# Eight-layer transformer on one core: zero rows in the nested projections, input by sequence, a late store of parts, and shifts split on GpSimd

## The chip, the cores and the metric

The kernel runs on one core of a Trainium2 chip as one program. The metric is its device time in microseconds (us), the median of several runs. The engines are PE (TensorE, matrix products), DVE (VectorE), ACT (ScalarE), POOL (GpSimd) and SP (SyncE, which issues the DMAs). In code and rows, "banks" are the eight PSUM banks that PE writes to.

## The reference

`x` holds 4 sequences of 1024 rows with 128 columns, float32. Eight layers follow one another, each `x = x + layer(layernorm(x))`: a causal attention with one head, a nested attention, a wide attention, the nested one again, a linear attention, a mixture of 8 experts, a gated recurrence and the mixture again. The change touches mostly the nested and the wide attention:

```python
def nested(x):                       # 8 heads of width 16
    for e in range(4):               # quarter e of the sequence sees m = 128, 64, 32, 16 features
        m = d // 2 ** e
        xm = layernorm(x[:, e*n:(e+1)*n])[..., :m] # with norm_w, norm_b
        q, k, v = xm @ q_w[:, :m].T + q_b, ...     # k_w, v_w the same way
    attn = softmax(q @ k.T * scale)  # all 1024 rows against all 1024 keys, per head
    out  = attn @ v                  # then xm @ o_w[:m, :m] + o_b[:m], the other columns 0
def wide(x):                         # 16 heads of width 8, no mask, no q, k, v bias
    q, k, v = x @ Wq.T / sqrt(D), x @ Wk.T, x @ Wv.T
    return softmax(q @ k.T) @ v @ Wff.T + bff
```

## The kernel before

**Frame.** `x` stays in SBUF from `load_stage` (L68, four DMAs at L73, one for each sequence) to `store_stage` (L91, four DMAs at L101). The main function runs the layers one after another. Every stage is a block of its own: an engine that enters a new block waits at a barrier until all five engines, SP among them, have left the block before.

**A layer with heads** (two nested, one wide) is three stages. `project_stage` (L413) handles the four sequences b in turn: DVE takes the statistics, POOL makes the factors of the layer norm in a chain of small instructions, DVE normalises (L545), PE turns the eight tiles (L687), ACT copies them back with norm_w and norm_b (L624), PE projects q and k (L697) and v (L704). Since float32 scores are wanted, q and k are cut into parts, two of type fp32r in the nested layers and three of type bf16 in the wide one (ACT L645 to L652, DVE L564 to L573), and SP writes the parts to DRAM (`store`, L474). In the nested layers each expert's matmuls use only m rows of weight and input: 128, 64, 32 and 16. ACT also scales `x` itself there (`grow_rows`, L635) and POOL adds the bias of the output (L519).

`attend_stage` (L717) reads the parts back, four heads (a group) at a time, to the rows of `q_stack` and `k_stack` (`Heads.load`, L398 and L402). A unit is one group and half of its rows: there are 16 units in each nested layer and 32 in the wide one, 64 in all. For a unit PE makes the plain scores (L896), DVE takes the maxima of two banks at a time (`maximum`, L797, 16 for each unit) and then the two bf16 parts of the negated row maximum (`shifts`, L804, L806, L808). PE turns these parts (`turn_shifts`, L905), ACT copies them out (L856), and SP moves them by four DMAs to two more rows of `q_stack` (L778), whose partners in `k_stack` are rows of ones. The shifted scores (L926) then come out less their maximum, ACT takes 32 exponentials (L849) and PE multiplies these with the values (L939). The maxima of a unit are taken while the exponentials of the unit before it run. `output_stage` applies the last weight (L1048 in PE).

**Order of the work.** Each engine's program is written out by hand in a fixed order, with semaphores between engines. SP issues load(0) and load(1) in the project stage after the stores of b = 0 and 1, then the stores of b = 2 and 3, and load(2) in the attend stage.

**The mixture layers** start with a chain on POOL (`Front.on_gpsimd`, L1105 to L1114), which makes the factor of the layer norm that is applied to an already normalised input.

## Time and profile before

| what | us |
|---|---|
| median of 3 runs (3285.5 to 3297.26) | 3286.0 |
| the profiled run, its own time | 3277.16 |
| its span | 3275.1 |
| load stage | 0 to 10.7 |
| first nested layer: project from, first scores at | 162.4, 245.0 |
| wide layer: project from, first scores at | 648.0, 712.8 |
| second nested layer: project from, first scores at | 1410.2, 1489.8 |
| first nested attend stage ends | 634.1 |
| mixture layers start | 2088.8 and 2851 |
| last addition ends, store is issued, span ends | 3264.6, 3265.9, 3275.1 |

PE is busy for 2907.9 us (89% of the span), DVE 2459.1, ACT 2215.6, POOL 188.5. The mean granted TensorE clock is 0.917 of full speed.

The views in the section of rows are of these kinds. In the page's clock line each digit is a slice of 81.9 us. A window row gives, for a stretch from:to, its length, then the busy time of PE, PE's weight loads, DVE, ACT and POOL, each with its number of instructions in brackets, then the granted clock, the busy share of the 16 DMA engines and GB/s. A timeline row gives start, duration, engine, line, operation and tiles with shapes and count; in brackets stands how long the engine was idle before it and what ended that. SPq is the time in which SP issues a DMA, PEld a weight load. A row by tile gives the shortest, median and longest duration in ns, and the first and last start.

### The profile page before, as it was taken

The numbers are of one execution on the slowest core, as the hardware profiler recorded it, in microseconds if no ns is written. First come the engines' busy times: TensorE is split into PE (matmuls) and PEld (weight loads), VectorE is DVE, ScalarE is ACT, GpSimd is POOL, SyncE is SP. The second block draws the span as 40 slices with busy tenths as digits, with TensorE's granted clock in tenths as the row PEclk, the third lists the DMA queues.
The fourth block names the chain that finished last, engine by engine and source line by source line (L and its number), as shares of the span: only waits on it lengthen the run. The fifth ranks groups of instructions, "written<-read, shape, count | busy, mean of one in ns | idle before, by whom it ended". The sixth has DMA issues, their size and how long they took to land. (4 is left out here: it accounts for less than half of the span.)

```text
span 3275.1 us, 53109 instructions
## 1 busy us (share of the span) xinstructions
PE 2907.9 (89%) x19734; PEld 1664.7 (51%) x19734; DVE 2459.1 (75%) x3887; ACT 2215.6 (68%) x3872; POOL 188.5 (6%) x329
## 2 busy tenths in 40 slices
PE   6868999859999999977999989799997777789998
PEld 4643444422333333353444456678885455578886
DVE  5648999479999999747999564477776777677776
ACT  2345888638888888953888722288886444378886
POOL 0030000020000000030000020100000000010000
PEclk9957999869999999966999989799998888889999
DMA  1052121030000000033221010211110000111112
GB/s 28 1 114 64 29 40 21 6 106 11 21 21 21 21 21 21 2 83 84 41 41 21 2 28 1 66 40 46 46 49 21 1 0 0 39 50 46 49 46 58
DMA packets 76838, 115.24 MB, mean 35 GB/s; under 512 B 13840, under 2 KB 38448, under 8 KB 76592
## 3 DMA queue, kind: packets, MB, share of 16 engines
q1 hardware_dynamic: 76592, 111.99, 14.5%
q8 instruction: 151, 2.47, 0.3%
q14 instruction: 95, 0.78, 0.1%
HBM read 85.73 MB, written 25.43 MB: 34 GB/s over the span
## 5 line engine op out<-in xcount | busy, mean ns | idle before, releaser
L797 DVE TENSOR_REDUCE nested_a_halves<-banks 128x2 f32<-128x1024 f32 x512 | 617.4, 1222 | 78.8 <-PE banks L896 75.6
L849 ACT ACTIVATE nested_a_p<-banks 128x512 f32<-128x512 f32 x1024 | 553.7, 597 | 117.1 <-PE banks L926 100.7
L797 DVE TENSOR_REDUCE wide_a_halves<-banks 128x2 f32<-128x1024 f32 x512 | 593.4, 1216 | 42.1 <-PE banks L896 42.1
L849 ACT ACTIVATE wide_a_p<-banks 128x512 f32<-128x512 f32 x1024 | 554.1, 598 | 44.5 <-PE banks L926 33.2
L1725 DVE TENSOR_TENSOR mix_e_h_low<-mix_e_h,mix_e_h_high 128x512 fp32r<-128x512 f32 x512 | 349.6, 688 | 174.9 <-ACT mix_e_h_high L1831 167.0
L1848 ACT ACTIVATE mix_e_h<-banks,mix_b_folded 128x512 f32<-128x512 f32 x512 | 353.8, 691 | 103.5 <-PE banks L1902 103.1
L939 PE MATMUL banks<-nested_a_p,nested_values 128*32 128x256 f32 x4096 | 326.9, 398 | 0.0
L939 PE MATMUL banks<-wide_a_p,wide_values 128*32 128x256 f32 x4096 | 321.0, 391 | 0.0
L1831 ACT ACTIVATE mix_e_h_high<-mix_e_h 128x512 fp32r<-128x512 f32 x512 | 319.3, 624 | 0.0
L896 PE MATMUL banks<-nested_k_stack,nested_q_stack 48*128 48x512 f32 x1024 | 270.8, 524 | 48.8 <-PEq L453 24.3
L926 PE MATMUL banks<-nested_q_stack,nested_k_stack 50*128 50x512 f32 x1024 | 252.3, 423 | 10.9 <-ACT nested_a_p L849 9.9
L926 PE MATMUL banks<-wide_q_stack,wide_k_stack 50*128 50x512 bf16 x1024 | 223.6, 381 | 22.6 <-ACT wide_a_p L849 19.3
L896 PE MATMUL banks<-wide_k_stack,wide_q_stack 48*128 48x512 bf16 x1024 | 205.9, 398 | 34.5 <-DVE wide_a_halves L797 18.1
L896 PEld LDWEIGHTS banks<-nested_k_stack,nested_q_stack 48*128 48x128 f32 x1024 | 102.0, 196 | 247.8 <-issue 186.7
L1902 PE MATMUL banks<-mix_x_high,mix_w_high 128*128 128x512 f32 x512 | 208.5, 407 | 0.0
L1916 PE MATMUL banks<-mix_e_h_high,mix_w_high 128*128 128x512 f32 x512 | 202.1, 395 | 6.9 <-DVE mix_e_h_low L1725 6.9
L1902 PE MATMUL banks<-mix_x_high,mix_w_low 128*128 128x512 f32 x512 | 205.1, 401 | 0.0
L1902 PE MATMUL banks<-mix_x_low,mix_w_high 128*128 128x512 f32 x512 | 203.3, 397 | 0.0
L1916 PE MATMUL banks<-mix_e_h_low,mix_w_high 128*128 128x512 f32 x512 | 203.3, 397 | 0.0
L1916 PE MATMUL banks<-mix_e_h_high,mix_w_low 128*128 128x512 f32 x512 | 201.1, 393 | 0.0
L926 PEld LDWEIGHTS banks<-nested_q_stack,nested_k_stack 50*128 50x128 f32 x1024 | 134.0, 190 | 67.6 <-ACT nested_a_p L849 47.4
L896 PEld LDWEIGHTS banks<-wide_k_stack,wide_q_stack 48*128 48x128 bf16 x1024 | 49.3, 93 | 232.6 <-issue 178.8
(365 smaller groups left out, 4190.2 us busy)
## 6 DMA issues: line engine op xcount, KB each, us to landing
mix_e_gate<-mix_gates_t SPq DMA_DIRECT2D x128, 256.0 KB, 3.2
nested_q_stack<-nested_q_parts SPq DMA_DIRECT2D x96, 128.0 KB
nested_q_parts<-nested_p_q_cut SPq DMA_DIRECT2D x16, 512.0 KB
nested_k_parts<-nested_p_k_cut SPq DMA_DIRECT2D x16, 512.0 KB
nested_k_stack<-nested_k_parts SPq DMA_DIRECT2D x32, 256.0 KB
wide_q_stack<-wide_q_parts SPq DMA_DIRECT2D x192, 32.0 KB
nested_k_stack<-nested_k_parts SPq DMA_DIRECT2D x32, 128.0 KB
mix_raw_w<-L_ffn_w_t SPq DMA_DIRECT2D x8, 512.0 KB, 7.2
```

What stands on the lines that cost most here:

```text
L797: dve.tensor_reduce(halves[:, half, i, 2 * a:2 * a + 2], bank[:, at:at + 2, :], AX, ALU.max).then_inc(maxed, 1)
L849: act.activation(p[:, kt % 4, j, :], bank[:, ST + n % RING, :], ACT.Exp, scale=scale).then_inc(probs, 1)
L896: last = pe.matmul(bank[:, at + h, :], q_stack[rows, slot(u), slab, q_at:q_at + P], k_stack[rows, slot(u), slab, half * BANK:(half + 1) * ...
L926: pe.matmul(bank[:, ST + n % RING, :], k_stack[rows, slot(u), slab, kt * P:(kt + 1) * P], q_stack[rows, slot(u), slab, u % 2 * T2:(u % 2 + ...
L939: last = pe.matmul(bank[32 * j:32 * j + 32, MIX, cols], hd.values[:, u // 2, kt, 32 * j:32 * j + 32], p[:, kt % 4, j, cols], start=(kt == ...
L1725: dve.tensor_tensor(h_parts[1][:, slot, :], h[:, slot, :], h_parts[0][:, slot, :].bitcast(F32), ALU.subtract).then_inc(cut, 1)
L1831: act.activation(h_parts[0][:, n % RING, :], h[:, n % RING, :], ACT.Copy).then_inc(high_cut, 1)
L1848: act.activation(h[:, n % RING, :], bank[:, HID + n % 4, :], ACT.Gelu, bias=mx.b1[:, n % STEPS:n % STEPS + 1]).then_inc(active, 1)
L1902: last = pe.matmul(bank[:, HID + n % 4, :], mx.w1[a][:, e, part_of * P:(part_of + 1) * P], mx.x_parts[b % 2 * 2 + half][:, c % 2 * BANK:(c ...
L1916: last = pe.matmul(bank[:, OUT + q % 2, :], mx.w2[a][:, s, :], h_parts[half][:, n % RING, :], start=(n % HC == 0 and k == 0), stop=(n % HC ...
```

## The change

The stages of projection:

- `load_stage` loads x[0] alone. The three other loads are issued in the causal stage behind its weights, each with a semaphore of its own, and DVE waits for them where it first needs them.
- A weight of the nested layers gets four copies, `[P, 4, D]`. Copy e has zeros in its rows from D >> e on (ACT, `keep_rows`, three instructions for each of four weights, with a column of ones and zeros that POOL makes in the load stage). All matmuls of the nested projections use all 128 rows, and so do those of the nested output stage.
- PE turns the next sequence between q, k and v of the present one. ACT, DVE and SP follow in a new order. The factor for DVE's normalising comes out of two instructions on POOL instead of seven; those that only `grow_rows` needs follow later.
- SP issues only load(0) and the stores of b = 0, 1 and 2 in the project stage. load(1) and, after the first unit's shifts, the stores of b = 3 and load(2) go to the attend stage. Each load waits for the parts of its own two sequences alone, and the waits for all parts at the start of the attend stage are gone.

The stages of scores: DVE makes only `top`, in two buffers, and POOL makes the two bf16 parts of it. The signs move to rows of minus one in `k_stack`. The first maximum of each unit waits for the `top` of the unit before it.

Elsewhere: the factor of the mixture layers takes two instructions on POOL instead of seven, and the second mixture layer stores `x` by chunks, with `store_stage` gone.

```diff
@@ load_stage @@
-            for b in range(B):
-                sp.dma_start(core.x[:, b * TILES:(b + 1) * TILES, :],
-                             x_dram[b].rearrange("(i p) d -> p i d", p=P)).then_inc(x_in, 16)
-            sp.wait_ge(x_in, 16 * B)
+            load_sequence(core, sp, x_dram, 0)
@@ causal_stage, SP behind its weights; DVE @@
+                for b in range(1, B):
+                    load_sequence(core, sp, x_dram, b)
+                dve.wait_ge(core.x_in[0], 16)
+                        if qt == 1 and first:
+                            for b in range(1, B):
+                                dve.wait_ge(core.x_in[b], 16)
@@ Heads.load @@
+        b, k = n // self.groups, n % self.SLOTS
+        sp.wait_ge(self.parts_out[b % 2], (b // 2 + 1) * 32 * self.parts)
@@ project_stage, SP @@
                 sp.wait_ge(ones_set, hd.SLOTS)
-                sp.wait_ge(parts_out[0], 32 * hd.parts)
-                for n in range(2):
-                    hd.load(sp, n)
-                for b in range(2, B):
+                hd.load(sp, 0)
+                for b in range(2, B - 1):
                     store(b)
@@ project_stage, GpSimd @@
+                def first_factor(b):
+
+                    power = core.minus_half[:, 0:TILES]
+                    scale, floor = (1.0 + LN_EPS, LN_EPS * LN_EPS) if masked else (1.0, LN_EPS)
+                    dst = both if masked else rstd
+                    pool.wait_ge(counted, (b + 1) * STATS)
+                    pool.tensor_scalar(padded[:, b], moments[:, b, :, 1], scale, floor, ALU.mult,
+                                       ALU.add).then_inc(factored, 1)
+                    pool.wait_ge(factored, b * FIRST + 1)
+                    pool.tensor_tensor(dst[:, b], padded[:, b], power, ALU.pow).then_inc(factored, 1)
@@ project_stage, ACT @@
+                def keep_rows(weight):
+
+                    for e in range(1, 4):
+                        act.activation(weight[:, e, :], weight[:, 0, :], ACT.Copy,
+                                       scale=core.keep[:, e:e + 1]).then_inc(kept, 1)
@@ project_stage, PE @@
                                 last = pe.matmul(bank[:, 2 + 2 * n + c, (lo - 4 * c) * P:(hi - 4 * c) * P],
-                                                 weight[0:m, :], h_t[0:m, b % 2, lo * P:hi * P], start=True, stop=True)
+                                                 weight[:, e, :], h_t[:, b % 2, lo * P:hi * P], start=True, stop=True)
                             last.then_inc(projected, 1)
+                    if b + 1 < B:
+                        turn(b + 1)
@@ attend_stage, SP @@
-                for k in range(2):
-                    sp.wait_ge(hd.parts_out[k], 16 * hd.parts * B)
-                hd.load(sp, 2)
+                hd.load(sp, 1)
                 for u in range(UNITS):
                     shift_load(u)
+                    if u == 0:
+
+                        for n in range(2):
+                            hd.store(sp, B - 1, n)
+                        hd.load(sp, 2)
@@ attend_stage, GpSimd @@
+                for u in range(UNITS):
+                    pool.wait_ge(top_made, u + 1)
+                    wait_past(pool, shift_turned, u)
+                    pool.tensor_copy(shift[:, :, 0, :], top[:, u % 2]).then_inc(high_made, 1)
+                    pool.wait_ge(high_made, u + 1)
+                    pool.tensor_tensor(shift[:, :, 1, :], top[:, u % 2], shift[:, :, 0, :], ALU.subtract).then_inc(shifts_made, 1)
@@ attend_stage, DVE @@
+                    if m == 0:
+                        wait_past(dve, top_made, u)
-                    wait_past(dve, shift_turned, u)
-                    dve.tensor_tensor(top[:], halves[:, 0], halves[:, 1], ALU.max).then_inc(top_made, 1)
-                    dve.wait_ge(top_made, u + 1)
-                    dve.tensor_scalar(shift[:, :, 0, :], top[:], -1.0, None, ALU.mult).then_inc(high_made, 1)
-                    dve.wait_ge(high_made, u + 1)
-                    dve.scalar_tensor_tensor(shift[:, :, 1, :], top[:], -1.0, shift[:, :, 0, :], ALU.mult,
-                                             ALU.subtract).then_inc(shifts_made, 1)
+                    wait_past(dve, shifts_made, u - 1)
+                    dve.tensor_tensor(top[:, u % 2], halves[:, 0], halves[:, 1], ALU.max).then_inc(top_made, 1)
@@ mixture_layer, SP @@
+                        if out_dram is not None and c and e == 6:
+                            store_chunk(c - 1)
```

SP around the end of the first nested project stage, before. L474 stores parts of q and k, L398 and L402 load a group back, the two branches are the end of the stage and the start of the next behind its barrier, and L778 moves the shifts:

```order
L402 DMA nested1_q_stack<-nested1_q_parts 16x2x1024
L474 DMA nested1_q_parts<-nested1_p_q_cut 8x16x1024 [waits nested1_p_rest_cut]
...
L474 DMA nested1_k_parts<-nested1_p_k_cut 8x16x1024
L453 UNCONDITIONAL_BRANCH
L768 UNCONDITIONAL_BRANCH [waits barrier_Pool_Activation_PE_DVE_SP_release]
L398 DMA nested1_k_stack<-nested1_k_parts 32x2x1024 [waits causal_projected,causal_ht_copied]
...
L778 DMA nested1_q_stack<-nested1_a_shift_rows 1x2x512 [waits nested1_a_shift_copied]
```

The same place on SP in the changed kernel (L400 stores parts, L411 and L415 load, L809 moves the shifts):

```order
L400 DMA nested1_k_parts<-nested1_k_cut 8x16x1024
L469 UNCONDITIONAL_BRANCH
L799 UNCONDITIONAL_BRANCH [waits barrier_Pool_Activation_PE_DVE_SP_release]
L411 DMA nested1_k_stack<-nested1_k_parts 32x2x1024 [waits causal_ht_copied]
...
L809 DMA nested1_q_stack<-nested1_a_shift_rows 1x2x512 [waits nested1_a_shift_copied]
L809 DMA nested1_q_stack<-nested1_a_shift_rows 1x2x512 x3
L400 DMA nested1_q_parts<-nested1_q_cut 8x16x1024 x2
L400 DMA nested1_k_parts<-nested1_k_cut 8x16x1024 x2
L411 DMA nested1_k_stack<-nested1_k_parts 32x2x1024 [waits causal_projected]
```

Behind the branch now stand load(1), the first unit's shifts, and then the stores of b = 3 and load(2), ahead of the second unit's shifts; eight stores stood between load(1) and the branch before, and four stand there now, behind load(0).

PE in the project stage, before, from the first turn on (L687 turns a tile of h, L697 projects q and k, L704 v):

```order
L687 MATMUL banks<-ident,nested1_p_h 128x128 [waits causal_probs,causal_qkv_copied]
...
L687 MATMUL banks<-ident,nested1_p_h 128x128 [waits causal_ln_steps,causal_probs]
L687 MATMUL banks<-ident,nested1_p_h 128x128 x3
L697 MATMUL banks<-nested1_p_h_t,nested1_p_wq 128x256 [waits causal_ln_steps]
L697 MATMUL banks<-nested1_p_h_t,nested1_p_wq 128x256 x3
L697 MATMUL banks<-nested1_p_h_t,nested1_p_wk 128x256 x4
L704 MATMUL banks<-nested1_p_wv,nested1_p_h_t 128x128 x8
```

And in the changed kernel (L715, L727 and L738):

```order
L715 MATMUL banks<-ident,nested1_p_h 128x128 [waits causal_probs]
L715 MATMUL banks<-ident,nested1_p_h 128x128 x3
L727 MATMUL banks<-nested1_p_h_t,nested1_p_wq 128x256 [waits nested1_p_kept,causal_ln_steps,causal_qkv_copied]
L727 MATMUL banks<-nested1_p_h_t,nested1_p_wq 128x256 x3
L727 MATMUL banks<-nested1_p_h_t,nested1_p_wk 128x256 x4
L715 MATMUL banks<-ident,nested1_p_h 128x128 [waits causal_ln_steps,causal_probs]
...
L738 MATMUL banks<-nested1_p_wv,nested1_p_h_t 128x128 [waits nested1_p_kept]
```

The turning of the second sequence stood ahead of the first q, and stands between the first k and the first v now. (Semaphores are named after the stage that first used them.)

DVE between two units of the first nested layer's attend stage, before (L797 is `maximum`, L816 and L821 write the mixed values):

```order
L797 TENSOR_REDUCE nested1_a_halves<-banks 128x2 [waits nested1_a_scored] x14
L804 TENSOR_TENSOR nested1_a_top<-nested1_a_halves 128x16 [waits nested1_a_shift_turned,nested1_a_maxed]
L806 TENSOR_SCALAR nested1_a_shift<-nested1_a_top 128x4x4 [waits nested1_a_top_made]
L808 SCALAR_TENSOR_TENSOR nested1_a_shift<-nested1_a_top,nested1_a_shift 128x4x4 [waits nested1_a_high_made]
L797 TENSOR_REDUCE nested1_a_halves<-banks 128x2 [waits nested1_a_scored] x2
L816 RECIPROCAL nested1_a_inverse<-banks 128x16 [waits nested1_a_written,nested1_a_mix_turned]
```

And in the changed kernel (L849 makes `top`, L842 is `maximum`):

```order
L842 TENSOR_REDUCE nested1_a_halves<-banks 128x2 [waits nested1_a_scored] x14
L849 TENSOR_TENSOR nested1_a_top<-nested1_a_halves 128x16 [waits nested1_a_shifts_made,nested1_a_maxed]
L842 TENSOR_REDUCE nested1_a_halves<-banks 128x2 [waits nested1_a_scored,nested1_a_top_made]
L842 TENSOR_REDUCE nested1_a_halves<-banks 128x2 [waits nested1_a_scored]
L856 RECIPROCAL nested1_a_inverse<-banks 128x16 [waits nested1_a_written,nested1_a_mix_turned]
```

Two of the three small instructions have left DVE, and the wait for `top_made` stands at the maximum that follows.

## Rows read from the trace of the kernel before

**Rows 1.** the page: granted TensorE clock in 40 slices of 81.9 us (tenths).

```profile
PEclk9957999869999999966999989799998888889999
```

**Rows 2.** windows, nested project: us, busy us by engine, clock, DMA share, GB/s.

```profile
205.00:219.00 14.00, 14.00 (x38) 9.04 (x38) 5.13 (x11) 12.10 (x24) 2.21 (x8) 0.50 0.73 200
...
232.00:245.00 13.00, 0.00 (x0) 0.02 (x1) 0.36 (x2) 0.00 (x0) 0.00 (x0) 0.50 0.57 150
```

**Rows 3.** timeline, end, and first shifts: start, us, engine, line [idle, releaser].

```profile
238.57 5.65 SPq L474 DMA_DIRECT2D nested_k_parts<-nested_p_k_cut  x2
...
245.01 1.22 PE L896 MATMUL banks<-nested_k_stack,nested_q_stack 48*128 48x512 f32 x4 [13.45 <-PEq L453]
...
268.06 2.87 SPq L778 DMA_DIRECT2D nested_q_stack<-nested_a_shift_rows  x4
```

**Rows 4.** timeline of its start.

```profile
165.25 0.24 POOL L492 TENSOR_SCALAR nested_p_padded<-nested_p_moments 128x8 f32<-128x8 f32 x1 [54.17 <-DVE nested_p_moments L536]
...
165.57 1.67 POOL L494 TENSOR_TENSOR nested_p_rstd<-nested_p_padded,minus_half 128x8 f32<-128x8 f32 x1
...
170.27 2.13 DVE L545 TENSOR_SCALAR nested_p_h<-x_resident,nested_p_moments,nested_p_both 128x128 f32<-128x128 f32 x8 [2.91 <-POOL nested_p_both L506]
...
179.83 4.21 PE L697 MATMUL banks<-nested_p_h_t,nested_p_wq 128*128 128x256 f32 x8
...
180.75 3.17 ACT L635 ACTIVATE x_resident<-x_resident,nested_p_fall,nested_p_grow 128x128 f32<-128x128 f32 x8
180.82 0.50 PEld L697 LDWEIGHTS banks<-nested_p_h_t,nested_p_wq 64*128 64x128 f32 x2 [0.65 <-issue]
```

**Rows 5.** windows, the same stage while load(0) is moved.

```profile
214.00:225.00 11.00, 11.00 (x29) 6.78 (x28) 3.76 (x7) 6.17 (x12) 2.20 (x8) 0.50 1.00 152
```

**Rows 6.** tile wq: SP issues it as both nested project stages start.

```profile
L458 SPq DMA_DIRECT2D nested_p_wq<-L_ffn_q_w_t x2: 328/347/366, 162.4 to 1410.2; - x2
```

**Rows 7.** timeline, first scores of the second nested and the wide layer.

```profile
1489.82 1.22 PE L896 MATMUL banks<-nested_k_stack,nested_q_stack 48*128 48x512 f32 x4 [10.82 <-PEq L453]
...
712.81 1.04 PE L896 MATMUL banks<-wide_k_stack,wide_q_stack 48*128 48x512 bf16 x4 [16.35 <-PEq L453]
```

**Rows 8.** windows of the wide project stage, the same columns.

```profile
663.80:670.60 6.80, 4.67 (x24) 3.04 (x23) 5.22 (x11) 3.33 (x5) 4.05 (x10) 1.00 0.00 0
670.60:674.00 3.40, 3.40 (x10) 2.08 (x10) 2.41 (x12) 1.97 (x3) 2.49 (x7) 0.50 0.74 231
```

**Rows 9.** timeline of the wide project stage.

```profile
648.01 0.36 SPq L458 DMA_DIRECT2D wide_p_wq<-L_attn_b_Wq_t  x1
...
664.66 1.88 PE L697 MATMUL banks<-wide_p_h_t,wide_p_wk 128*128 128x512 f32 x4
...
701.11 1.21 DVE L573 TENSOR_TENSOR wide_p_k_cut<-wide_p_rest,wide_p_k_cut 128x1024 bf16<-128x1024 f32 x1
```

**Rows 10.** timeline, start and end of the kernel; last line, landings by tile.

```profile
11.40 1.65 DVE L128 BATCH_NORM_STATS2 causal_ln_stats<-x_resident 128x6 f32<-128x128 f32 x8 [11.40 <-POOL causal_above L183]
...
3263.93 0.69 DVE L1754 TENSOR_TENSOR x_resident<-x_resident,banks 128x512 f32<-128x512 f32 x1 [0.75 <-PE banks L1927]
3265.89 3.91 SPq L101 DMA_DIRECT2D out<-x_resident  x4
...
DMA to landing us min/median/max: 3.3/5.8/7.0
```

**Rows 11.** timeline inside one unit of the wide layer.

```profile
774.33 0.18 DVE L804 TENSOR_TENSOR wide_a_top<-wide_a_halves 128x16 f32<-128x16 f32 x1
...
774.85 2.35 DVE L797 TENSOR_REDUCE wide_a_halves<-banks 128x2 f32<-128x1024 f32 x2
...
776.12 0.39 PE L905 MATMUL banks<-ident_bf,wide_a_shift 128*8 128x128 bf16 x4 [0.17 <-DVE wide_a_halves L797]
```

**Rows 12.** groups by line: turning the shifts (busy, mean ns | idle before).

```profile
L905 PE MATMUL banks<-ident_bf,wide_a_shift 128*8 128x128 bf16 x128 | 12.6, 222 | 6.1 <-DVE wide_a_halves L797 6.0
```

**Rows 13.** timeline, first mixture layer: DVE beside GpSimd.

```profile
2110.70 2.73 DVE L1697 TENSOR_TENSOR mix_r_equal<-mix_r_equal,mix_r_earlier 128x512 f32<-128x512 f32 x1
```

More of the change, by code:

```diff
@@ L611, in _, with constant @@
             def _(act):
-                def ones(dst, shape):
+                def constant(dst, shape, value):
                     source = core.ident[:, 0:1].unsqueeze(2).broadcast_to([P] + shape)
-                    return act.activation(dst, source, ACT.Identity, bias=core.one[:], scale=0.0)
+                    return act.activation(dst, source, ACT.Identity, bias=value[:], scale=0.0)
                 def copy_turned(b):
@@ L865, in _ @@
                 copy_shifts(0)
-                for k in range(2):
-                    act.wait_ge(hd.parts_out[k], 16 * hd.parts * B)
                 for u in range(UNITS):
@@ L2309, in program @@
             lambda: recurrent_stage(core, recurrent),
-            lambda: mixture_layer(core, "mix2", mixture),
+            lambda: mixture_layer(core, "mix2", mixture, out),
         ]
```

191 lines of the change are left out of this document (99 added, 92 removed).

## The prediction, made before the changed kernel had run

> **What bounds the kernel now.** I read the page's clock line first, then windows of each project stage, the timeline where each stage hands over to the next, and last one unit of the attend stages in single rows. All sums are made against the profiled run's own 3277.2 us, which lies 8.8 us under the median of the runs, 3286.0; I add these 8.8 at the end. For scale, 0.5% of this kernel is 16 us, about what a measurement can tell from no change.
>
> The clock line falls to 5 or 6 in the slices that hold the project stages [rows 1]. In the first nested one PE is busy for all of 14.00 us and is granted 0.50 of full speed, the lower of its two levels (1.2 of 2.4 GHz); later 13 us pass in which no engine computes and the DMA engines move 150 GB/s [rows 2]. The reader is to see there that this stage has two bounds one behind the other. PE at half clock is the first. The second is SP: it issues the last store of parts from 238.57 to 244.2, and PE's first scores, at 245.01, had waited 13.45 us for the block to end [rows 3]. The second nested and the wide stage end alike, with idle of 10.82 and 16.35 us [rows 7]. In the attend stages PE sets the pace, with a short wait for DVE in each wide unit [rows 11, 12].
>
> **The nested project stages.** From the stage's start at 162.4 [rows 6] to the first scores at 245.0 [rows 3] are 82.6 us; from 1410.2 [rows 6] to 1489.8 [rows 7] are 79.6.
>
> *Start.* The first q matmul stands at 179.83, 17.4 us in. DVE's normalising waited 2.91 us for the chain of seven on POOL; two instructions give the factor at 165.57 + 1.67 = 167.2, against 170.2 [rows 4]. The turning of the second sequence, whose normalising came 6.5 us behind the first, no longer stands ahead of q. Against this ACT adds six copies of 128 columns for wq and wk, 3.17 / 8 = 0.40 us each [rows 4], 2.4 us in all, on the path. I take q at 10 us in, 7 us earlier.
>
> *PE.* A group of eight passes takes 4.21 us at half clock, with idle of 0.65 us in front of the loads of another row count [rows 4]. The same columns with 128 rows throughout took 1.88 us in the wide stage [rows 9], in which the clock was at 1.00 with PE busy for 4.67 of 6.80 us, but at 0.50 in the piece behind it with PE busy for all 3.40 [rows 8]. Rows of zero make the nested matmuls like the wide ones. At full clock a sequence is 3 x 1.9 + 1 = 6.7 us of PE; at half clock 3 x 3.5 + 2 = 12.5 (3.5 lies between 4.21 less two idle stretches, 2.9, and twice 1.88). Four sequences, less the first turn, end at 10 + 27 - 1 = 36 us in the one case and 10 + 50 - 2 = 58 in the other. On the way ACT has its own work, some 8 to 9 us a sequence with `grow_rows` (3.17), which puts a floor near 46 us.
>
> *DMA.* The first scores need load(0), which needs the stores of b = 0 and 1. A store of a sequence is four DMAs of 512 KB, 2.1 MB, and load(0) 1.6 MB: 5.8 MB. At 152 GB/s [rows 5] that is 38 us, at the 200 of [rows 2] 29. The first store can start once q and k of b = 0 are cut, some 4.5 us behind the first q: 14.5. So load(0) lands between 43.5 and 53 us in. I take 53 since the queue is full throughout as in rows 5. The stores of b = 3, load(1) and the wait for all parts no longer stand in front.
>
> The latest is then DMA at 53, plus 0.6 for the barrier: 53.6. Nested 1 gains 82.6 - 53.6 = **29.0** and nested 2 79.6 - 53.6 = **26.0**. Bounds: 49 (ACT, with a faster DMA) and 59 (PE at half clock) give 33.5 to 23.5 and 30.5 to 20.5.
>
> **The wide project stage** has 128 rows already. It runs from 648.01 [rows 9] to the first scores at 712.81 [rows 7], 64.8 us. DVE's last cut ends at 702.3, 54.3 us in [rows 9]; after it only SP's issues of stores are left. These go to the attend stage, so 54.3 + 0.6 = 54.9: **9.9**, between 6 (the new order makes ACT or DVE later) and 14 (earlier, as the second turning is out of the way).
>
> **Start and end.** DVE begins at 11.40, when all four loads have landed; one load lands after 3.3 at the least and 5.8 at the median of all [rows 10]. Issued at 0.8, x[0] is there at about 5.1: **6.3** (5 to 7). The copies of `keep` on POOL are over before. At the end the last addition ends at 3264.6, the four stores are issued at 3265.89 and the span ends at 3275.1 [rows 10], 10.5 us behind the addition. One chunk needs one issue and 3.3 us: **7.1** (5 to 8). The seven chunk stores ahead of it lie between gate loads on SP, with nothing late behind them that the trace shows: nothing, at most 2 us lost.
>
> **Units.** In the wide layer PE's turning of the shifts waits for DVE's first maximum behind `shifts` [rows 11], 6.0 us over 32 units [rows 12]. DVE's three small instructions take 0.52 us (774.33 to 774.85); with one and its own wait I expect 0.2 to 0.3. So **6** are gained, at most 0.31 x 31 = 10, at least nothing. Nested units have no such wait: nothing. The first unit of each layer gains the same 0.3, **1** for three. The parts now come from POOL. Its price here is not in the trace: two instructions over 128x16. The nearest rows from below are POOL's 0.24 on 128x8, from above its pow, 1.67 [rows 4]; DVE took 0.18 for `top` [rows 11]. I take 0.25 to 0.3, since neither is a power; with two hand-overs of 0.1 to 0.2 the parts are there 0.65 to 0.95 us behind `top`, at 775.2 to 775.5. PE turns at 776.12 now and could from about 775.9. So the chain is hidden by 0.4 to 0.7 us of scores, and what exceeds this costs its whole length in every unit, since shift rows and their DMAs follow.
>
> **Small ones.** The shorter chain of the mixture layers, 3 us less on POOL, meets weights that land soon behind it: 1 each, **2** (0 to 5). The output stages of the nested layers lose their changes of row count, four sequences with 0.3 us each at full clock: **1** each (0 to 2), 2.
>
> **Sum:** 29.0 + 26.0 + 9.9 + 6.3 + 7.1 + 6 + 1 + 2 + 2 = 89.3. 3277.2 - 89.3 = 3187.9; with the 8.8 the forecast is **3196**. The ends: 60 saved give 3226, 114 give 3172.
>
> **Rivals.**
>
> *B, the clock stays at half in the nested project stages.* For it speaks that PE was already busy without a gap there and got 0.50 [rows 2], and that the wide stage fell to 0.50 in its densest piece [rows 8]. Against it speaks the 1.00 of rows 8 just before. PE then ends at 58 us, DVE's copy of v and the barrier add 1.5, the first scores stand at 59.5: 5.9 more for each, 12, **3208**. The Trainium skill ("TensorE: Matmul & The Clock Gate", Part 1) lets the clock be set by how busy PE has recently been, whatever the rows it uses. By that rule alone zero rows change nothing in the clock; the 0.50 with PE busy for 14.00 of 14.00 us [rows 2] does not agree with it, so this case decides by its runs.
>
> *B2, rows do not matter at all*, neither for the clock nor for the 0.65 us of idle. A group then stays at 4.3 us, PE ends at 10 + 12 x 4.3 + 6 = 67.6, the scores start at 69: gains of 13.6 and 10.6, 31 us less than my sum, **3227**. For it speaks that the loads of 64 rows take no less than others; against it the idle stretches [rows 4]. The Trainium skill (same page, "Step-by-step: what each phase is for") says that a weight load's time goes by its columns and that rows don't matter; the 0.65 us [rows 4] does not agree with it.
>
> *C, the moved transfers.* At the start of attend, the store of b = 2 (2.1 MB) and load(1) (1.6 MB) lie ahead of the first shifts, 25 us at 150 GB/s; these are issued 23.0 us in now (245.01 to 268.06) [rows 3]. Then the stores of b = 3 and load(2), 3.7 MB, another 25 us, stand ahead of the second unit's shifts, which are wanted one unit later, some 22 us (a sixteenth of what is left of the attend stage's 389 us). Both are close: 2 to 3 us late each, 5 in each of three stages, 15: **3211**, up to 10 a stage, 3226.
>
> *D, the other side: POOL's two instructions.* If each costs like pow, the parts come at 774.51 + 0.1 + 1.67 + 0.1 + 1.67 = 778.05, 2.1 us too late. Each of the 61 inner units of three layers pays that: 128 us, and the kernel takes **3324**, slower than before. It decides from 90 / 61 = 1.5 us behind PE's need, that is parts 2.9 us behind `top`. Also for it: DVE's 512-column instruction took 2.73 us beside POOL [rows 13]. Against it: POOL's 0.24 [rows 4], and that DVE's maxima read the banks. The Trainium skill ("SBUF — State Buffer", the terms) names a port pair that DVE and GpSimd take in turns, each for a whole instruction; rows 13 agree, and no row of before shows it beside a maximum.
>
> *E, the change does not do what it says*: the first scores still come behind all stores, because the transfers share one queue, so that only the 7 us at each nested start stay, with 6.3 + 7.1 + 6 + 1 + 2 + 2 elsewhere: 38 us, **3248**.
>
> **How the numbers follow.** My case 0.58, B 0.14, B2 0.06, C 0.15, D 0.03, E 0.04. The likeliest gives 3196. Its own bounds, 3172 to 3226, hold B and C; B2 asks for 3228. D and E stay outside: 3170 to 3228. Slower by over 0.5% is D alone, 0.03; within 0.5% would be a mild D, 0.02; faster 0.95.
>
> **What would show it.** First scores 49 to 59 us behind the start of each nested project stage, with no computing-free stretch of 10 us before them; the clock of that stage at 1.00 in pieces and PE's weight loads without the 0.65; a wide stage 55 us long; DVE's first instruction near 5 us; the span's end some 4 us behind the last addition; parts of the shifts under 1 us behind `top`, and the wide turning without its wait. I am wrong if the units of the attend stages grow, if PE idles before the first shifted scores of a layer or of its second unit, or if load(0) lands later than 55 us in.

## The result, and the profile after

The changed kernel takes **3168.1 us** in the median of four runs (3166.4 to 3176.2), the kernel before 3291.6 (3285.5 to 3300.3). The ratio is 0.963, with a 95% interval from 0.960 to 0.966. I had said 3196, between 3170 and 3228: the direction was right, and the time lies 1.9 us under the lower end. In the profiled runs the span went from 3275.1 to 3164.3, by 110.8 us, where my terms came to 89.3.

The page of the changed kernel, its head and its clock line (as rows 1):

```profile
span 3164.3 us, 53194 instructions
...
PE 2853.7 (90%) x19734; PEld 1646.9 (52%) x19734; DVE 2438.1 (77%) x3759; ACT 2219.3 (70%) x3896; POOL 187.9 (6%) x398
...
PEclk9969999979999999968999899799998888889999
```

The first nested project stage runs from 156.3 to the first scores at 207.2. Windows of it, with the columns of rows 2: length, busy time by engine, granted clock, DMA share, GB/s.

```profile
175.00:185.00 10.00, 8.06 (x47) 7.15 (x46) 8.04 (x23) 10.00 (x23) 5.37 (x16) 0.95 0.50 186
185.00:196.00 11.00, 11.00 (x65) 9.77 (x64) 4.14 (x8) 9.53 (x18) 4.40 (x16) 0.89 0.66 242
196.00:207.00 11.00, 0.04 (x1) 0.00 (x0) 4.05 (x8) 6.51 (x13) 2.19 (x8) 0.73 0.66 134
```

PE is granted 0.95 and 0.89 where rows 2 had 0.50, and PE is idle for the last eleven microseconds, in which the DMA engines move 134 GB/s (150 to 200 in rows 2 and 5). The timeline of the same stage names what came last (as rows 3 and 4):

```profile
166.38 3.75 PE L727 MATMUL banks<-nested_p_h_t,nested_p_wq 128*128 128x256 f32 x8 [2.28 <-ACT nested_p_h_t L638]
...
171.67 1.34 SPq L400 DMA_DIRECT2D nested_q_parts<-nested_q_cut  x2
...
197.95 1.26 ACT L659 ACTIVATE nested_q_cut<-banks,nested_p_q_bias 128x512 fp32r<-128x512 f32 x2 [3.42 <-DMA nested_k_parts<-nested_k_cut]
...
207.16 1.22 PE L934 MATMUL banks<-nested_k_stack,nested_q_stack 48*128 48x512 f32 x4 [11.12 <-DMA nested_q_stack<-nested_q_parts]
```

The first q stands 10.1 us into the stage (I said 10), the first store 15.4 (14.5). ACT's cut of b = 3 waits for the store of b = 1 to leave its buffer, and PE's first scores wait for a DMA of load(0), no longer for the end of the block. So the bound is the one I had named, at 50.9 us where I had 53.6. The margin is small: SP's first issue behind the block's end stands at 206.17, 1.0 us before these scores, so compute, held up by that buffer, ends almost as late as the DMA.

The wide project stage, first q, last cut and first scores (as rows 9 and 7):

```profile
609.15 3.75 PE L727 MATMUL banks<-wide_p_h_t,wide_p_wq 128*128 128x512 f32 x4 [0.78 <-ACT wide_p_h_t L641]
...
644.25 1.22 DVE L587 TENSOR_TENSOR wide_k_cut<-wide_p_rest,wide_k_cut 128x1024 bf16<-128x1024 f32 x1
...
646.15 1.04 PE L934 MATMUL banks<-wide_k_stack,wide_q_stack 48*128 48x512 bf16 x4 [7.33 <-PEq L469]
```

Here lies the largest miss: the stage started at 600.54 and took 45.6 us, and I had 54.9.

One wide unit (as rows 11), and the row by tile of ACT's copies of the shift rows, one for each of the 32 units, with the first and the last start:

```profile
707.14 0.18 DVE L849 TENSOR_TENSOR wide_a_top<-wide_a_halves 128x16 f32<-128x16 f32 x1
707.35 2.36 DVE L842 TENSOR_REDUCE wide_a_halves<-banks 128x2 f32<-128x1024 f32 x2
707.38 0.20 POOL L830 CAST wide_a_shift<-wide_a_top 128x16 bf16<-128x16 f32 x1 [19.72 <-DVE wide_a_top L849]
...
707.66 0.22 POOL L832 TENSOR_TENSOR wide_a_shift<-wide_a_top,wide_a_shift 128x16 bf16<-128x16 f32 x1
...
708.63 0.39 PE L943 MATMUL banks<-ident_bf,wide_a_shift 128*8 128x128 bf16 x4
...
L896 ACT ACTIVATE wide_a_shift_rows<-banks x32: 586/586/586, 667.9 to 1295.1; 8x512 bf16<-8x512 f32 x32
```

POOL's two instructions take 0.20 and 0.22 us and end 0.56 us behind `top`, of which I had expected 0.65 to 0.95. PE turns them without a wait: over the 32 units it idles 0.9 us before the turning, and 6.1 before the change. The units follow each other at (1295.1 - 667.9) / 31 = 20.23 us, where the kernel before had 20.51. DVE's maxima beside POOL take 1218 ns in the mean, against 1216 before, so no hold by POOL shows in them.

The start, and the end (as rows 10):

```profile
4.98 1.65 DVE L125 BATCH_NORM_STATS2 causal_ln_stats<-x_resident 128x6 f32<-128x128 f32 x8 [4.98 <-DMA x_resident<-L_attn_a_x]
...
3160.21 0.69 DVE L1800 TENSOR_TENSOR x_resident<-x_resident,banks 128x512 f32<-128x512 f32 x1 [0.75 <-PE banks L1973]
3160.93 0.39 SPq L1657 DMA_DIRECT2D out<-x_resident  x1
```

DVE begins at 4.98 (5.1 forecast), and the span ends 3.4 us behind the last addition, where it had been 10.5.

Stage by stage, from first instruction to first instruction, in the profiled runs:

| stretch | before | after | gained | forecast |
|---|---|---|---|---|
| up to the first nested stage | 162.4 | 156.3 | 6.1 | 6.3 |
| nested 1, project to first scores | 82.6 | 50.9 | 31.8 | 29.0 |
| nested 1, attend and output | 403.0 | 393.4 | 9.6 | 1.3 |
| wide, project to first scores | 64.8 | 45.6 | 19.2 | 9.9 |
| wide, attend and output | 697.4 | 691.5 | 6.0 | 6.3 |
| nested 2, project to first scores | 79.6 | 50.1 | 29.5 | 26.0 |
| nested 2, attend, output, linear | 598.7 | 601.3 | -2.6 | 1.3 |
| mixture 1, recurrence | 762.4 | 761.1 | 1.3 | 1.0 |
| mixture 2 and the end | 424.1 | 414.3 | 9.9 | 8.1 |

### The profile page after: what moved, and what is told of

Read it like the earlier page. It is cut to its first block and busy times, and to the rows that moved or that the text cites. A ratio compares the mean times of both kernels' runs of the same rounds, so it can differ in the third digit from the quotient of the medians.

```text
span 3164.3 us, 53194 instructions
## 1 busy us (share of the span) xinstructions
PE 2853.7 (90%) x19734; PEld 1646.9 (52%) x19734; DVE 2438.1 (77%) x3759; ACT 2219.3 (70%) x3896; POOL 187.9 (6%) x398
## 5 line engine op out<-in xcount | busy, mean ns | idle before, releaser
L842 DVE TENSOR_REDUCE nested_a_halves<-banks 128x2 f32<-128x1024 f32 x512 | 613.1, 1222 | 74.0 <-PE banks L934 70.8
L842 DVE TENSOR_REDUCE wide_a_halves<-banks 128x2 f32<-128x1024 f32 x512 | 593.9, 1218 | 33.3 <-PE banks L934 32.2
L889 ACT ACTIVATE wide_a_p<-banks 128x512 f32<-128x512 f32 x1024 | 554.3, 598 | 45.6 <-PE banks L964 34.2
L977 PEld LDWEIGHTS banks<-nested_a_p,nested_values 128*32 128x32 f32 x4096 | 85.2, 109 | 155.7 <-issue 89.1
```

The costliest lines, as they stand in the source:

```text
L842: dve.tensor_reduce(halves[:, half, i, 2 * a:2 * a + 2], bank[:, at:at + 2, :], AX, ALU.max).then_inc(maxed, 1)
L889: act.activation(p[:, kt % 4, j, :], bank[:, ST + n % RING, :], ACT.Exp, scale=scale).then_inc(probs, 1)
L977: last = pe.matmul(bank[32 * j:32 * j + 32, MIX, cols], hd.values[:, u // 2, kt, 32 * j:32 * j + 32], p[:, kt % 4, j, cols], start=(kt == ...
```

## The experiments

Twelve experiments ran, (8) being the changed kernel again. They are compared stage by stage in their profiles; in the profiles whose edit does not touch them, the nested project stages repeat to 1.0 us (49.9 to 50.9) and the wide one to 1.1 (45.4 to 46.5). A whole run of one and the same kernel varies by more than 15 us. A time given as "the run took" is a single run and is too rough to price an edit by. "First scores" is always the time from the project stage's start.

**The rows (1).** The edit, in q, k, v and the output:

```diff
-                                                 weight[:, e, :], h_t[:, b % 2, lo * P:hi * P], start=True, stop=True)
+                                                 weight[0:m, e, :], h_t[0:m, b % 2, lo * P:hi * P], start=True, stop=True)
```

> The changed kernel, but every matmul of the nested projections and outputs uses only its m rows (128, 64, 32, 16) again; the copies with zero rows are still made. If zero rows lift the clock and remove the idle ahead of loads of another row count, the nested project stages fall back to about half clock with weight loads that wait 0.65 us, q, k and v take 4.3 us each, PE ends some 62 to 68 us into the stage, and the first scores stand at 63 to 70 instead of 50.9 and 50.1: 24 to 38 us longer in all. If it is the new order alone (the rival that rows do not matter), they stay at 50 to 52. Wide project 45.6 and units 21.78 and 20.22 in any case.

Windows of the first nested project stage, and one of its weight loads:

```profile
175.00:185.00 10.00, 10.00 (x33) 7.19 (x32) 4.90 (x15) 7.04 (x13) 6.20 (x17) 0.50 0.50 169
185.00:196.00 11.00, 11.00 (x38) 7.36 (x37) 6.25 (x16) 7.12 (x16) 0.00 (x0) 0.60 0.41 127
196.00:207.00 11.00, 11.00 (x36) 7.64 (x35) 3.67 (x6) 7.82 (x15) 2.20 (x8) 0.56 0.88 198
...
187.00 0.50 PEld L727 LDWEIGHTS banks<-nested_p_h_t,nested_p_wk 64*128 64x128 f32 x2 [0.65 <-issue]
```

The first scores came at 65.8 and 68.3 us, and the run took 3224.4. PE is busy for 10.00, 11.00 and 11.00 us and is granted 0.50, 0.60 and 0.56, where the changed kernel has 0.95 and 0.89 for the same products with less busy time. The wait of 0.65 us at the load of 64 rows is back. This is no accident of one run. In every profile with 128 rows, (5) among them, the clock stands at 1.00 for 5 us or more in both nested project stages. In the three profiles with m rows (the kernel before, (1) and (12)) it rises at most once in a stage, for 3 to 4 us, and falls back while PE stays busy. So rivals B and B2 fall: zero rows lift the clock. Whether it is the rows themselves or the waits that go away with them is not separated, since the edit changes both; the waits are the smaller part, as a group of eight at a clock of 0.50 takes 3.75 us with 128 rows (at 166.38) and 4.2 to 4.3 with m rows. The output stages, PE's part of which takes 8.87 us in the changed kernel, took 11.3.

**The order of compute (2).** PE turns the first two sequences ahead of q and each later one behind v; ACT and DVE follow their old order.

```diff
-                    if b + 1 < B:
-                        turn(b + 1)
...
                 turn(0)
+                turn(1)
                 for b in range(B):
                     project(b)
+                    if b + 2 < B:
+                        turn(b + 2)
```

> The changed kernel with the old order of PE, ACT and DVE in all three project stages (both first turnings ahead of q, grow_rows ahead of the cuts, normalising behind cut_last); zero rows, POOL's two instructions and SP's order stay. My theory for the wide stage, whose first scores came at 45.6 us where I had 54.9: the order alone brought it, so it returns to 53 to 55. The rival, SP's shorter list or the higher clock brought it: it stays at 46 to 48. The nested stages are bound by DMA once the first store starts; the first store starts some 5 us later and the first scores come 3 to 6 us later, 54 to 57.

The wide project stage began at 606.67:

```profile
620.75 3.62 PE L729 MATMUL banks<-wide_p_h_t,wide_p_wq 128*128 128x512 f32 x4
...
660.69 1.22 DVE L587 TENSOR_TENSOR wide_k_cut<-wide_p_rest,wide_k_cut 128x1024 bf16<-128x1024 f32 x1
...
662.22 1.03 PE L937 MATMUL banks<-wide_k_stack,wide_q_stack 48*128 48x512 bf16 x4 [6.97 <-PEq L469]
```

First scores at 55.6 us in the wide stage: with SP's new list and the old order, my 54.9 for it was right to 0.7. What I had not priced is the order, 9.9 us. In the nested stages, 58.4 and 59.1, it is worth 7.6 and 9.0, more than the 3 to 6 expected. The run took 3184.0.

**The turning alone (11).** Only the turning of PE and its copies on ACT in the old order.

> The changed kernel with only the turning in the old order (PE turns both first sequences ahead of the first q and each later one behind v; ACT copies them at the matching places); ACT's and DVE's other orders are the new ones. With the whole old order the wide stage took 55.6 us and the nested ones 58.4 and 59.1, against 45.6, 50.9 and 50.1. If the turning alone is what the new order brings, 53 to 56 in the wide stage and 57 to 60 in the nested ones; if it is ACT's and DVE's order, 46 to 49 and 50 to 53. In between, the 5.5 us of the later first q (14.1 against 8.6) are the turning's, and the 4.5 behind it belong to ACT and DVE: 51 in the wide stage, 55 in the nested ones, which I hold likeliest.

The wide project stage began at 605.86:

```profile
619.92 3.30 PE L728 MATMUL banks<-wide_p_h_t,wide_p_wq 128*128 128x512 f32 x4
...
659.94 1.04 PE L936 MATMUL banks<-wide_k_stack,wide_q_stack 48*128 48x512 bf16 x4 [7.43 <-PEq L469]
```

54.1 us in the wide stage, 57.0 and 57.3 in the nested ones. Of the ten, the turning is 8.5; the 1.5 left for ACT's and DVE's order are little more than the 1.1 by which this stage differs between profiles. My likeliest case, 51 and 55, was wrong: the later start of q (5.5 us) is not all of the 8.5. I take it that later sequences find their turned input late as well; no row here shows it. The run took 3192.2; in its last nested unit the clock fell.

**SP's list (3).**

```diff
                 hd.load(sp, 0)
-                for b in range(2, B - 1):
+                hd.load(sp, 1)
+                for b in range(2, B):
                     store(b)
```

> The changed kernel with SP's old list: load(1) and the stores of b = 3 in the project stage, waits for all parts and load(2) at the head of the attend stage. If the queue is what bounds the nested project stage, 11.6 MB at 150 to 160 GB/s from 15 us on, less what is still in flight at the end, put the first scores at 68 to 78 us instead of 50.9: 35 to 50 us longer for both. If the matmuls were the bound and the list matters little, 51 to 56. Wide: 10 us later if the stores of b = 3 are late, 46 if not.

The first scores of the first nested layer:

```profile
220.99 1.22 PE L932 MATMUL banks<-nested_k_stack,nested_q_stack 48*128 48x512 f32 x4 [26.96 <-PEq L469]
```

First scores at 66.3 and 64.3 us in the nested stages, 57.1 in the wide one; the run took 3208.6. In the first of them v ended at 39.3 us (39.8 in the changed kernel), and PE then waited until 66.3. The list is worth 15.4, 14.2 and 11.5 us. It came 2 to 4 us under the range that I had set for the nested stages.

**SP's list without the rest (12).** Both edits of (1) and (2) at once: of the project stages only SP's list and the shorter chain are new.

> The changed kernel with m rows and the old order of compute together, so that of the project stages only SP's list and the two-instruction factor are new. Bounds one behind the other: PE at half clock, which ended v at 69 us before, ends it at 65 to 69 again, and the first scores follow within 2 to 3 us, at 68 to 72 in the nested stages: SP's list alone brings 10 to 13 of the 32 and 29 us. If the parts add up as they were taken away one by one (15 rows, 8 order, 15 SP's list, of 32), 73 to 75. Wide: 55.6, since only the order was taken back there.

```profile
222.45 1.22 PE L937 MATMUL banks<-nested_k_stack,nested_q_stack 48*128 48x512 f32 x4 [1.11 <-PEq L469]
```

First scores at 66.95 in both nested stages, v ending at 65.8, and 55.5 in the wide one; 3216.6. It is 1 us under the range. The first scores follow PE by 1.1 us. With m rows the new order brings nothing: (1), which has it, stands at 65.8 and 68.3. What POOL's shorter chain brings by itself was not tried.

**The rows without the rest (5).** The kernel before with the copies and all 128 rows, nothing else.

> The kernel before with the zero rows alone (copies of the weights on ACT, all matmuls of the nested projections and outputs with 128 rows); order, chains and SP's list are the old ones. Theory: rows, order and SP's list each bring little alone, since the stage has several bounds one behind the other; PE gets faster, v ends 10 to 18 us earlier than at 69, but SP's eleven and a half MB still end the stage, so the first scores come at 68 to 76 instead of 82.6 and 79.6. Rival, the parts add up (rows brought 15 and 18 when taken away from the changed kernel): 62 to 67. Rival, rows need the new order: 78 to 83. The output stages of the nested layers take 1.6 us less in any case but the last.

SP's last two stores of the first nested stage and the first scores:

```profile
220.48 12.82 SPq L480 DMA_DIRECT2D nested_q_parts<-nested_p_q_cut  x2
233.34 5.45 SPq L480 DMA_DIRECT2D nested_k_parts<-nested_p_k_cut  x2
...
239.58 1.22 PE L918 MATMUL banks<-nested_k_stack,nested_q_stack 48*128 48x512 f32 x4 [24.69 <-PEq L459]
```

77.2 and 74.8 us, 5.5 and 4.8 less than before, although v ended at 52.5 and 51.3, some 17 us earlier. PE then waits 24.69 us for SP, which is held in its issue of a store for 12.82 us. The run took 3276.8. The rows are worth 5 us alone, 15 and 18 with the rest: the stage has three bounds, one behind the other: SP's list (77.2 us here, 66.3 in (3)), PE with m rows (65.8 to 68.3) and the DMA of load(0) with the stores ahead of it (50.9).

**DVE makes the parts (4).** The three instructions back on DVE, nothing on POOL.

> The changed kernel with DVE making both bf16 parts of the shifts in three instructions, no POOL in the attend stages. If the units became shorter by what DVE no longer does, they return to 22.0 (nested, 21.78 now) and 20.5 us (wide, 20.22 now), 15 us in all. If they became shorter by something else, they stay at 21.78 and 20.22.

```profile
L890 ACT ACTIVATE wide_a_shift_rows<-banks x32: 586/586/586, 669.7 to 1305.4; 8x512 bf16<-8x512 f32 x32
```

(1305.4 - 669.7) / 31 = 20.51 us a wide unit, and 22.01 a nested one, as before the change; 3170.9. So both steps of 0.28 and 0.23 us come from what DVE no longer does. In the whole time the 15 us do not show: 3170.9 is a single run, 2.8 us over the changed kernel's median. In the nested units I had seen no wait. It was there one instruction further on: PE's plain scores behind the turning, in the eight steady units of a window. The group of the kernel before, then of the changed one, then of (4):

```profile
L896 PE MATMUL banks<-nested_k_stack,nested_q_stack 48*128 48x512 f32 x256 | 63.4, 491 | 1.1
```

```profile
L934 PE MATMUL banks<-nested_k_stack,nested_q_stack 48*128 48x512 f32 x256 | 63.1, 490 | 0.0
```

```profile
L928 PE MATMUL banks<-nested_k_stack,nested_q_stack 48*128 48x512 f32 x252 | 62.2, 490 | 1.1
```

1.1 us of idle before L896 in eight units, 0.14 each, none after, and 1.1 again with the three instructions back on DVE. The other 0.09 of the 0.23 us are not in this row.

**POOL made slower (6).** Six more small instructions ahead of the two.

```diff
+                    pool.tensor_copy(spare[:], top[:, u % 2]).then_inc(spared, 1)
+                    pool.wait_ge(spared, 6 * u + 1)
```

> The changed kernel with six more small instructions on POOL in every unit, ahead of the two that make the parts of the shifts, each waiting for the one before: about 6 x 0.28 = 1.7 us more between top and the parts (0.56 now, 2.3 then). PE's turning stands 1.3 us behind top's end now, so the parts are about 1.0 us late. If lateness costs its whole length in every unit, as I priced it, the units grow by 0.8 to 1.1 us, to 22.7 and 21.2, 55 to 65 us in all. If the shift rows have slack behind the turning, the units grow by less than 0.3. If POOL's instructions hold DVE beside them, DVE's maxima grow and the units by more than 1.3.

The turning's group (32 units), and the tile of the shift rows:

```profile
L956 PE MATMUL banks<-ident_bf,wide_a_shift 128*8 128x128 bf16 x128 | 12.5, 220 | 27.5 <-POOL wide_a_shift L845 27.5
...
L909 ACT ACTIVATE wide_a_shift_rows<-banks x32: 587/587/587, 683.1 to 1332.1; 8x512 bf16<-8x512 f32 x32
```

The parts came 2.12 us behind `top`, and PE turned them at 2.27, in place of 1.31: 0.96 late. The wide units took (1332.1 - 683.1) / 31 = 20.94, 0.71 more, the nested ones 22.44, 0.65 more; 3208.7. Three quarters of the lateness count in the wide units, so rival D was priced nearly right and was far off in its condition. The parts are there 0.75 us before PE turns them; they came 1.56 us later here and cost PE 0.96, so 0.60 of it was slack.

**Three buffers (7), and the changed kernel again (8).**

```diff
-        self.cuts = [core.sbuf(ctx, n, [P, 2, self.parts, T], kind) for n in ("q_cut", "k_cut")]
+        self.cuts = [core.sbuf(ctx, n, [P, 3, self.parts, T], kind) for n in ("q_cut", "k_cut")]
...
                 store(0)
-                store(1)
                 sp.wait_ge(ones_set, hd.SLOTS)
                 hd.load(sp, 0)
+                store(1)
```

> The changed kernel with three buffers for the cut parts in place of two, and load(0) issued right behind the store of b = 0, which is all it needs, ahead of the store of b = 1. In the nested stages DMA (three transfers, 5.8 MB, from 15.4 us in) ended last at 50.9; two transfers, 3.7 MB, end some 23 us behind 15.4, at 39, and the cuts of b = 3 no longer wait for the store of b = 1, so that compute ends near 43 to 45. First scores at 43 to 46 in both nested stages: 10 to 14 us less in all; wide stays at 45.6. Rival: the queue is as full as before and what is moved comes back as late shift rows or a late load(1): nothing gained in the sum.

> The changed kernel itself, on the same chip as the run with three buffers. 3166 to 3176. If the clock's rise at the head of each attend stage is a matter of phase, it comes at other places than 46, 36 and 62 us behind the first scores; if it is fixed by the program, at the same.

SP and PE at the end of the first nested project stage of (7):

```profile
197.94 6.13 SPq L400 DMA_DIRECT2D nested_k_parts<-nested_k_cut  x2
...
204.86 1.22 PE L934 MATMUL banks<-nested_k_stack,nested_q_stack 48*128 48x512 f32 x4 [8.70 <-PEq L469]
```

First scores at 48.5 and 47.7 us: 2.4 less each than in the changed kernel's first profile, 1.6 and 2.4 less than in its repetition (50.1 and 50.1), and not the 5 to 7 expected. Compute was through 45.9 us in, but now the block ends with SP, held for 6.13 us in its issue of the store of b = 2; the next step would be to move that store too, which was not tried. That load(0) could go ahead of the store of b = 1 at all shows that it waits for the parts of b = 0 alone: each load of a nested layer needs one sequence. In the time this can't be seen: 3161.5 us (3152.9 to 3178.5, six runs) against 3163.7 (3156.0 to 3173.6, five) for the changed kernel on the same chip, ratios to the kernel before 0.9624 [0.9594, 0.9654] and 0.9618 [0.9591, 0.9645]. In the repetition the clock rose some 45, 36 and 38 us behind the first scores of the three layers: at the same place in the first two, and 24 us earlier in the third.

**Idle matmuls for the clock (9 and 10).**

```diff
+                    if u == 0 or (u == 1 and m < PAIRS // 2):
+                        for i in range(3):
+                            pe.matmul(bank[:, MIX, i * P:(i + 1) * P], core.ident_bf[0:128, :],
+                                      core.ident_bf[0:128, :], start=True, stop=True)
```

> The changed kernel with three idle matmuls of 128 columns and 128 rows (the identity by itself, into a bank that is overwritten later) behind every pair of plain scores at the head of each attend stage, up to the first shifted scores. PE is busy for 0.80 of every 1.13 us there at half clock and waits for DVE. Theory from the rows experiment: what the clock answers to is the activity of the array's rows, 48 in the scores. Then these matmuls bring the clock to full within the first 20 us instead of 36 to 62, PE's part of unit 0 runs at full clock, and each attend stage gets 4 to 17 us shorter, 20 to 35 us in all: 3130 to 3145. Rival, the rise is a matter of time or phase: it still comes at 36 to 62 us, and the kernel stays at 3160 to 3170, or 3 us slower where PE is late for DVE.

> The same with idle matmuls of 32 rows, same columns and count, so that PE is as busy as in the kernel with 128. If rows count, the clock rises later than there, at 36 to 62 us as in the changed kernel, and the time is 3160 to 3175. If PE's busy time counts and not its rows, both kernels show the same early rise and the same time.

Windows of the kernel with 128 rows, behind the first scores at 207.1:

```profile
222.10:237.10 15.00, 14.42 (x64) 6.51 (x64) 14.04 (x14) 0.59 (x1) 0.41 (x2) 0.50 0.13 24
237.10:252.10 15.00, 15.00 (x77) 6.44 (x75) 9.42 (x8) 8.88 (x17) 0.00 (x0) 0.50 0.80 203
```

PE is busy for 14.42 and then 15.00 of 15.00 us and stays at 0.50. The clock rose 48, 38 and 42 us behind the first scores of the three layers, with 32 rows at 42, 40 and 52. The times are 3171.2 us (3166.5 to 3185.3), ratio 0.9656 [0.9632, 0.9681], and 3162.0 in a single run. So matmuls of 128 rows in this share do not bring the clock up: from 207 to 252 us the added ones take 12.1 us of PE and the plain scores 26.2. A larger share was not tried.

## Why the prediction was right and wrong

**What held.** The two bounds of the nested stage, PE at half clock and SP's list, were the right ones, and taking both away left the third, the DMA of 5.8 MB: 50.9 and 50.1 us, where I had 53.6. It moved in 35.5 us (171.7 to 207.2) where I had 38, from 0.9 us later on. My reason for the store of b = 1 in this sum was wrong and its price right: load(0) doesn't need it (7), it only stood ahead of it in SP's list. The clock reached 1.00 in pieces, and the waits of 0.65 us went. The start (6.1 for 6.3), the end (7.1 for 7.1), the stretch with the first mixture's front (1.3 for 1) and the wide units (31 x 0.28 = 8.7, inside 0 to 10, for 6) came about as worked out. That the table has 6.0 for the wide attend stage where I had 6.3 is luck: from the last shift rows to the next stage it took 42.5 us in place of 39.5, at a granted clock of 0.83 to 0.95 in place of 1.00. In the nested output stages PE's part fell from 10.49 to 8.87 us, 1.6 in each layer where I had 1.

**The step that failed most: the wide project stage.** I put "DVE's last cut ends at 702.3, 54.3 us in [rows 9]; after it only SP's issues of stores are left" and kept the 54.3. That treats the compute as fixed while the change reorders it. Experiments (2) and (11) show the price: 9.9 us for the order, 8.5 of them for the turning. The rows to see it were there. In the nested stage I had taken 7 us for the same turning ahead of q, and the wide stage's first q stood 14.1 us in, as against 17.4. I carried the term into two of three stages that run the same function, and gave it only the upper bound of 14 in the third; 19.2 were gained.

**The second: nested units.** "Nested units have no such wait: nothing" was read from the turning's rows alone. DVE's 0.3 us showed in part at the next instruction, L896, and cost 0.23 us a unit: 2.8 us in each layer (263.9 to 261.1 over twelve units). Experiment (4) takes it back.

**The third: the offset to the median.** I added 8.8 us, as if the profiled run of the kernel before stood to its median as the next one would to its own. It was the fastest of all its runs, 3277.2 at a mean clock of 0.917. Eleven later runs on one chip took 3280.6 to 3299.8 at 0.916 to 0.907. The changed kernel's profiled run, 3166.4, lies 1.7 under its median of 3168.1. So 8.8 - 1.7 = 7.1 us of my miss of 27.9 are this. (The sum was 3196.7 and stands as 3196.) The other 21 are terms: 9.3 in the wide project stage, 6.3 in the nested ones, 5.6 in the nested units, 2.7 in the wide ones, 1.8 in the second mixture and the end, 1.2 in the nested output stages, 26.9 in all, less 6.0 that the clock took away, half of it in the nested layers and half at the end of the wide one.

**Rival C** did not come: the first shifts of nested 2 were issued at 1410.45, and the first shifted scores stood at 1416.44, 6.0 us later as before. The second unit's shifts of nested 1 were issued at 255.64, as soon as ACT had copied them (255.02 and 0.59 us). **E** fell with the result itself, the first scores standing ahead of the stores of b = 3, and **B** with experiment (1); **D** fell with POOL's 0.20 and 0.22 us. On B, the Trainium skill ("TensorE: Matmul & The Clock Gate", Part 1) lets the clock follow how busy PE has been and names no rows there; (1) does not agree, with 0.50 to 0.60 at 100% busy against 0.89 to 0.95 at 81 to 100%, for the same products. On **B2**, the same page ("Step-by-step: what each phase is for") says that rows don't matter to a weight load; the duration of a load agrees, but the 0.65 us of idle before one of another row count does not, and it came back with the m rows. Between the loads of 32 and of 16 rows no wait stands, before the change or in (1).

**The range.** Its lower end was the sum of all upper bounds, 114 us, for a wide stage of at most 14 and nested units of nothing. The time lies 1.9 us beyond it; the 19.2 of the wide stage, the 5.6 of the nested units or the 7.1 of the offset would each have been enough to hold it. A bound on a term that was never worked out can't hold the time.

## What to carry to other kernels

Where a change reorders a function that runs in several stages, price the order in each of them, and don't keep the end of compute fixed where only its tail is discussed. Bounds one behind the other don't add: the rows were worth 5 us alone and 15 with the rest, so an edit that looks useless alone may be the one that lets the others pay. A wait that an engine causes may be recorded at an instruction behind the one that is looked at: read the idle time of the instructions that follow too.

## What the runs showed of the hardware

The granted clock depended on what PE computed, not only on how busy it was. The same projections with 16 to 128 rows ran at 0.50 [rows 2] and at 0.50 to 0.60 (1), with one rise of 3 to 4 us at the most in a stage, and with zeros in the missing rows at 0.89 to 0.95; the waits between loads of different row counts went in the same edit. But 128-row matmuls of the identity among scores of 48 rows changed nothing (9). What in the array counts is open: the identity, like the scores, leaves most of it without data, but so do zero rows. Added matmuls of dense data, or more of them, were not tried.

At the head of each attend stage the clock stays at 0.50 and then rises for good, 36 to 66 us behind the first scores; for the last 7 us at the least of that time, and for 36 at the most, PE is busy without a pause. The time can differ between runs of one program. Two windows of the second nested layer of the changed kernel (first scores at 1387.7), and one of its repetition (first scores at 1383.0):

```profile
1433.00:1443.00 10.00, 10.00 (x60) 3.59 (x64) 5.27 (x5) 4.92 (x9) 0.34 (x2) 0.50 0.23 35
1443.00:1453.00 10.00, 10.00 (x72) 3.55 (x70) 6.14 (x6) 5.73 (x11) 0.00 (x0) 0.63 0.00 0
```

```profile
1428.30:1438.30 10.00, 9.91 (x96) 4.22 (x98) 8.59 (x8) 8.07 (x16) 0.00 (x0) 1.00 0.25 36
```

The clock rose 62 us behind the first scores in the first and 38 in the second; the first two units took 27.7 and 26.2 us, against 22.8 and 21.7. Likewise, from ACT's copy of the last unit's shift rows to PE's first turning in the output stage a nested layer took 29.1 us, and 34.2 to 38.7 where the clock fell on the way (34.2 in the first nested layer before). Such moments may be most of the spread between runs, for the time goes with the mean clock: the changed kernel took 3156.0 us at 0.936, 3163.7 at 0.935 and 3173.6 at 0.931 on one chip. It is not shown, since these runs have no profiles. In the table "nested 1, attend" gained 9.6 and "nested 2, attend" lost 2.6 through the same: 5.1 of the 9.6 are the last unit's (34.2 to 29.1), and 8.1 were lost in the first two units of nested 2 (45.9 to 54.0). What sets the moment stays open.
